# Cross attention: GpSimd adds the four key tiles, and TensorE's one pass of denominator products follows the step's value products

## What is computed

```python
def _attention(x, ctx, wq, wk, wv, wo, bo):      # 20 heads of 64, ctx is (8, 512, 256)
    q = (x @ wq).reshape(B, N, HEADS, DHEAD).transpose(0, 2, 1, 3)
    k = (ctx @ wk).reshape(B, M, HEADS, DHEAD).transpose(0, 2, 1, 3)
    v = (ctx @ wv).reshape(B, M, HEADS, DHEAD).transpose(0, 2, 1, 3)
    sim = jnp.einsum('bhid,bhjd->bhij', q, k) * SCALE
    attn = jax.nn.softmax(sim, axis=-1)
    out = jnp.einsum('bhij,bhjd->bhid', attn, v)
    out = out.transpose(0, 2, 1, 3).reshape(B, N, INNER)
    return out @ wo + bo
...
x = x + _attention(n, context, a2_wq, a2_wk, a2_wv, a2_wo, a2_bo)      # n: layer norm of x
```

## Time and profile before

| | us |
|---|---|
| median of 3 runs | 1702.72 |
| lowest and highest | 1698.43, 1707.77 |
| the profiled execution's own time | 1697.7 |
| its span, first to last instruction | 1695.9 |
| TensorE busy | 1550.1 (91%) |
| VectorE busy | 1033.5 (61%) |
| ScalarE busy | 778.9 (46%) |
| GpSimd busy | 450.1 (27%) |

### The profile page before, as it was taken

The page is one execution under the profiler, slowest core; times in us unless marked ns, Lnnn a source line. Parts: engine busy times, 40 slices in busy tenths (PEclk is TensorE's granted clock), DMA queues, the critical chain, the costliest instruction groups (busy, mean ns, idle before and its releaser), DMA issues. The chain is left out here.

```text
span 1695.9 us, 41168 instructions
## 1 busy us (share of the span) xinstructions
PE 1550.1 (91%) x18128; PEld 1220.5 (72%) x18128; DVE 1033.5 (61%) x1417; ACT 778.9 (46%) x1061; POOL 450.1 (27%) x399
## 2 busy tenths in 40 slices
PE   4999999985899999999589999999999999999678
PEld 3556666543788888887467888788787888787478
DVE  3577777754676777666455555565656555545176
ACT  2466666643454544454344344344444444434133
POOL 3333333202222322222213223232323323323100
PEclk8599999976999999999799999999999999999789
DMA  4332221100200000000201000000010000000100
GB/s 134 114 107 61 60 66 41 37 2 24 87 2 2 2 2 2 2 2 2 73 1 27 2 26 2 26 2 26 2 26 2 21 7 2 2 2 2 42 12 19
DMA packets 26779, 45.52 MB, mean 27 GB/s; under 512 B 7344, under 2 KB 15472, under 8 KB 26224
## 3 DMA queue, kind: packets, MB, share of 16 engines
q1 hardware_dynamic: 26176, 39.03, 7.9%
q10 hardware_dynamic: 432, 3.93, 0.6%
HBM read 29.51 MB, written 1.31 MB: 18 GB/s over the span
## 5 line engine op out<-in xcount | busy, mean ns | idle before, releaser
L1046 DVE TENSOR_REDUCE a_negmax<-a_pscore 128x2 f32<-128x1024 f32 x160 | 195.6, 1223 | 113.0 <-PE a_pscore L821 113.0
L1621 DVE TENSOR_REDUCE l_negmax<-l_pscore 128x2 f32<-128x154 f32 x320 | 203.2, 684 | 66.7 <-PE l_pscore L1326 65.9
L973 ACT ACTIVATE raw_weights<-a_pst 128x1024 f32<-128x1024 f32 x160 | 164.0, 1025 | 164.5 <-PE a_pst L846 163.8
L1508 ACT ACTIVATE l_probs<-l_pst 128x1024 f32<-128x1024 f32 x160 | 163.9, 1025 | 103.3 <-PE l_pst L1341 103.3
L1119 POOL TENSOR_TENSOR raw_weights<-raw_weights 128x512 f32<-128x512 f32 x80 | 106.7, 1337 | 341.4 <-ACT raw_weights L973 341.4
L692 POOL TENSOR_TENSOR a_key_sum<-a_probs 128x1024 f32<-128x1024 f32 x40 | 96.2, 2405 | 240.8 <-ACT a_probs L568 240.8
L870 PE MATMUL a_pj<-a_ct,a_wk 64*128 64x512 f32 x960 | 130.4, 404 | 4.8 <-DVE a_ql L1034 3.8
L625 DVE TENSOR_REDUCE a_negmax<-a_pscore 128x4 f32<-128x1024 f32 x80 | 97.7, 1221 | 57.5 <-PE a_pscore L445 57.5
L1119 POOL TENSOR_TENSOR a_key_sum<-raw_weights 128x512 f32<-128x512 f32 x80 | 102.6, 1285 | 102.7 <-ACT raw_weights L973 102.7
L880 PE MATMUL a_pj<-a_wv,a_ct 128*128 128x256 f32 x960 | 126.2, 288 | 3.1 <-DVE a_kl L1034 3.1
L880 PEld LDWEIGHTS a_pj<-a_wv,a_ct 128*128 128x128 f32 x960 | 118.9, 191 | 3.8 <-issue 2.9
(11 more groups left out here) (212 smaller groups left out, 3348.7 us busy)
## 6 DMA issues: line engine op xcount, KB each, us to landing
l_ct<-in_ctx_t SPq DMA_DIRECT2D x8, 512.0 KB, 4.0
l_k_stack<-l_k_hi SPq DMA_DIRECT2D x64, 64.0 KB, 2.1
a_ct<-in_ctx_t SPq DMA_DIRECT2D x8, 512.0 KB, 4.7
a_ct<-in_ctx_t SPq DMA_DIRECT2D x16, 256.0 KB, 5.2
l_q_stack<-l_q_hi SPq DMA_DIRECT2D x80, 32.0 KB, 1.9
l_x<-in_x_t SPq DMA_DIRECT2D x8, 256.0 KB, 4.1
l_k_stack<-l_k_lo SPq DMA_DIRECT2D x32, 64.0 KB, 2.1
raw_weights<-in_a_wv ACTq DMA_DIRECT2D x1, 1920.0 KB, 11.3
```

The costliest lines, as they stand in the source:

```text
L973: nc.scalar.activation(probs[:, 2 * i:2 * i + 2, 2 * n:2 * n + 2, :], pst[:].rearrange("p h (k q) -> p h k q", k=2), ACT.Exp, scale=SCALE) ...
L1046: nc.vector.tensor_reduce(to, pscore[:], AX.X, ALU.max, negate=True).then_inc(max_done, 1)
L1508: nc.scalar.activation(probs[:, g % 2, 2 * pair:2 * pair + 2, 2 * n:2 * n + 2, :], pst[:].rearrange("p h (k q) -> p h k q", k=2), ACT.Exp, ...
L1621: last = nc.vector.tensor_reduce(to[:, :, k], pscores[s % 2][:, :, keys], AX.X, ALU.max, negate=True)
```

## The change

It has three parts, all in `cross_attention_layer`:

- GpSimd: behind each of the two adds of tiles 2+3 it waits for that add (half_summed) and adds the result onto `key_sums[0]`, in place; sum_ready is now set by these two new adds alone. GpSimd makes six adds of 128x512 in a step, where it made four.
- TensorE: the denominators are one pass of four products instead of two passes, and they leave `weighted_sums` for a function of their own that runs at the very end of the turn, behind `values(d)`.
- VectorE: `normalise` moves from the end of turn d to the beginning of turn d + 1: behind `low_queries`, in front of the layer norm's low half and of `maximum` slot 1.

```diff
@@ TensorE
-                for n in range(2):
-                    pe.wait_ge(sum_ready, 4 * e + 2 * n + 2)
-                    for t in range(4):
-                        last = mm(pv[t * 32:(t + 1) * 32, SQ:2 * SQ], ones[:], key_sums[n][:, t, :],
-                                  start=n == 0, stop=n == 1)
+
+            def denominators(e):
+
+                for i in range(2):
+                    pe.wait_ge(sum_ready, 2 * e + i + 1)
+                    for t in (2 * i, 2 * i + 1):
+                        last = mm(pv[t * 32:(t + 1) * 32, SQ:2 * SQ], ones[:], key_sums[0][:, t, :],
+                                  start=True, stop=True)
                 last.then_inc(pv_done, 1)
...
                     values(d)
+                if here(d - 2):
+                    denominators(d - 2)
@@ VectorE
                         if here(d):
                             low_queries(d)
+                        if here(d - 3):
+                            normalise(d - 3)
                         if next_norm(d, LN_SPLIT):
                             ln.dve_lo(dve, next_norm(d, LN_SPLIT), nt)
...
                 if here(d):
                     low_keys(d)
-                if here(d - 2):
-                    normalise(d - 2)
@@ GpSimd
                         nc.gpsimd.tensor_tensor(key_sums[n][:, two], probs[:, two, 2 * n, :],
-                                                probs[:, two, 2 * n + 1, :], ALU.add).then_inc(sum_ready, 1)
+                                                probs[:, two, 2 * n + 1, :], ALU.add).then_inc(half_summed, 1)
+                        if n == 1:
+                            pool.wait_ge(half_summed, 4 * e + 3 + i)
+                            nc.gpsimd.tensor_tensor(key_sums[0][:, two], key_sums[0][:, two], key_sums[1][:, two],
+                                                    ALU.add).then_inc(sum_ready, 1)
```

More of the change, by code:

```diff
@@ L762, in cross_attention_layer @@
         st_ready, exp_done = sem("st_ready"), sem("exp_done")
-        sum_ready = sem("sum_ready")
+        half_summed, sum_ready = sem("half_summed"), sem("sum_ready")
         pv_done, recip_done, ot_ready = sem("pv_done"), sem("recip_done"), sem("ot_ready")
```

## The result

| | before | after |
|---|---|---|
| median, us | 1700.58 (4 runs) | 1800.31 (4 runs, 1789.8 to 1806.47) |
| span of the profiled execution, us | 1695.9 | 1796.1 |

The changed kernel takes 1.0577 times as long, 95% interval 1.0511 to 1.0644, which is 87 to 110 us more. 1811 was predicted, in a range from 1768 to 1840.

What follows compares the result with a forecast made beforehand. TensorE's own stream was taken as the bound, busy 198.2 of 200 us. Products -12.8, GpSimd 0, stall +85.7 and clock +35 sum to +107.9 us; on the median 1702.7 that gave 1811 us, range 1768 to 1840.

Steps and rivals of the forecast that it cites:

- TensorE's products: Denominators on TensorE: one pass fewer in 40 turns, less an extra change of tile shape; 12.8 us gained, between 8.4 and 17.2.
- the extra change of tile shape: TensorE's denominators, now between values and next score, enter 32 columns once more per turn: 0.11 us, 4.4 us in all.
- GpSimd: Two more adds per step on GpSimd, 103 us of work on an engine idle for 70%: cost zero.
- the cover by the values: GpSimd's last sum is ready 2.8 us before TensorE asks behind the values; 0.5 us margin in one turn of five.
- The stall: TensorE's score waits for slot 1's maximum behind normalise: 2.21 us in 31 turns, 2.46 in 7, 85.7 us in all.
- the wake-up: TensorE's waiting weight load for the score starts 0.06 us behind the end of VectorE's maximum.
- The clock: TensorE's clock falls behind the new gaps: 26 falls at 1.36 us, 35 us, between 0 and 63.
- the 7 long gaps: TensorE idle about 3.0 us in turns with the layer norm's low half; three falls in four expected, 5 in all.
- the 31 short ones: TensorE idle about 1.9 us in the other turns with the stall; two falls in three expected, 21 in all.
- The page's rule: Rival: the stall is there but the clock holds in nearly all turns, 1776 us; chance 0.24 for 1768 to 1790.
- normalise is hidden: Rival: slot 1's maximum is ready when TensorE asks, leaving only TensorE's gain, 1690 us; chance 0.04.
- GpSimd is late: Rival: TensorE's denominators wait for GpSimd's adds, about 1850 us; chance 0.06 for above 1840, shared with both bounds at upper ends.

Runs made afterwards that it cites:

- e_norm_only: The kernel before with only normalise moved behind a_ql in the next turn, denominators and GpSimd's four adds as before: 1808.90 us.
- e_two_passes: The kernel after with GpSimd's four adds and two passes of products with ones again, both passes behind the values: 1827.24 us.
- e_filler: The kernel after plus seven unneeded TensorE products in front of the score of slot 2 in each of 38 turns: 1770.87 us.
- e_split: The kernel after with normalise cut into three operations: reciprocal before a_ql, products behind the maxima of slots 1 and 2: 1696.33 us.
- e_halves: The kernel with halves: e_split with the reciprocal in two halves, before a_ql and behind slot 1's maximum, both products behind slot 2's: 1684.88 us.

## Why the prediction was right

- **TensorE's products.** 0.32 us a turn were forecast: 0.43 for the pass, 0.11 for the extra change of tile shape. In turns without a fall e_norm_only and the kernel after, between which this is TensorE's only difference, lie 0.29 to 0.31 us apart, so it is some 12 us for the layer against 12.8. The pass itself was 0.43, as e_two_passes shows; 0.12 to 0.14 is left for the change of tile shape. The kernel with halves has hardly a stall, and its layer is 9.4 us shorter than before.
- **GpSimd.** Forecast at zero. Its last sum came 3.6 us ahead of TensorE's question in the turn shown, and in the waits after TensorE never waits for it. In the old place it was waited for 24.1 us, so the cover by the values, which the prediction named, was needed and was enough.
- **The stall.** The reciprocal to the next maximum took 2.45 us (2.46 forecast); the wake-up took 0.05 (0.06). Between the kernel before and e_norm_only turns without a fall are 2.1 to 2.2 us longer (2.21 forecast), and the 7 with the layer norm's low half 2.3, where the prediction had the full 2.46. That makes about 83 us against 85.7. In e_filler, where the clock is at 1.00, the layer is 788.5 - 711.7 = 76.8 us longer than before, some 3 us of it the filler's own, against 85.7 - 12.8 = 72.9 forecast.
- **The clock.** The step was right; that its size came so close is partly luck. 26 falls at 1.36 us were forecast, 35 us; the trace has 22 at 1.5, 33 us: too many were taken, at too low a price. By kind, the 7 long gaps, from which five falls were expected, were followed by none, and the 31 short ones by 22, where 21 were expected. The number itself hangs on more than the gap: the same gaps were followed by 15 falls in e_norm_only and 26 in e_two_passes, 23 to 39 us, and the rows of the kernel before don't tell which. The range covered all of these.
- **The page's rule.** By the Trainium skill ("TensorE: Matmul & The Clock Gate", section "HAM oscillation — how this bites in real kernels") gaps as short as these leave the clock alone; by that rule the time was 1776 us. The trace does not agree: gaps of 1.9 us by the matmuls' modelled ends were followed by falls, and without them, in e_filler, the time is 1771 us. The rival was priced well and did not come about.
- **The sum.** -12.8 + 85.7 + 35 = +107.9 was forecast; the terms as measured are about -12 + 83 + 33 = +104, and the layer grew by 106.8 us. About half of what is between is one more fall, in turn 1; the kernel before has it ahead of its first score. (The prediction took from turn 1 that the clock holds there; in the kernel after it reads 0.51 from 859.5 to 863.0, in that turn.) The median grew by 99.7. In the profiled executions the rest of the program was 6.6 us shorter: 1796.1 - 818.5 = 977.6 us against 1695.9 - 711.7 = 984.2. The forecast lies 8 us above this, inside the measurement's interval of 87 to 110 us.
- **The other rivals.** That normalise is hidden (1690 us) did not come about where the change puts it, and e_split and e_halves show that it can be had by another place. That GpSimd is late did not come about either.

## What to carry to other kernels

When work moves on an engine that is idle 40% of the time, its busy share says nothing: look for the first thing behind the new place that the bounding engine waits for, and how much slack that had. Here it was 0.18 us for an operation of 2.46, and the same work cut into pieces that fit idle times of 1.26, 0.95 and 0.76 us cost about 2 us in the whole layer. A stall on TensorE can cost more than its own length, because the clock may fall behind it; keeping TensorE busy in the gap shows how much of a loss is the clock's. And where the clock falls in some turns only, compare turns of the same kind in which it did not: a difference of 0.3 us shows there, when in the whole layer it was hidden behind seven falls more or fewer.

## What the runs showed of the hardware

Seven products that nobody needs, put into a gap of TensorE, made the kernel 29 us faster (1800.31 to 1770.87). The falls of the clock don't follow the length of the gap alone: in the kernel after it fell behind 2.26 and 2.36 us and held behind 3.22 us, in the same turns of each batch; with turns 0.43 us longer (e_two_passes) it was low at the end of the gap of 3.23 us in five batches of seven. The same gaps were followed by 15, 22 and 26 falls in three kernels, at about 1.5 us each. What decides it in a turn is not shown. The reciprocal of 128 rows took 0.55 us for 64 columns, 0.95 for 128 and 1.75 for 256, so cutting it into two halves costs 0.15 us.
